# Three plain scatters and one accumulating scatter in each group of a message stream, on one NeuronCore

## What is computed

```python
h = jnp.maximum(_layernorm(x, axis=-1), 0.0)
x = x + _L0_gnn_ref(h, edge_index, W_l, W_r, b)          # mean over neighbours, two products, log-softmax
h = jnp.maximum(_layernorm(x, axis=-1), 0.0)
# second layer
weight = jnp.maximum(edge_rbf @ W1 + b1, 0.0) @ W2 + b2  # one row of 128 for each edge
hl = h @ Wl + bl
row, col = (edge_index[0], edge_index[1])                # row = src, col = dst
msg = hl[col] * weight
x = x + jax.ops.segment_sum(msg, row, num_segments=x.shape[0])
```

## Time and profile before

| | us |
|---|---|
| median of 3 runs | 3699.18 |
| the profiled execution's own time | 3703.27 |
| span of its trace (first to last instruction) | 3701.4 |
| first scatter starts | 1046.68 |
| last scatter starts | 3589.90 |
| POOL busy in the whole span | 2207.1 |

### The profile page before, as it was taken

One profiled execution on the slowest core, in us unless ns is written; L12 is line 12 of the kernel. 1 busy time (PEld: TensorE's weight loads), 2 busy tenths in 40 slices (PEclk: granted clock), 3 DMA queues, 4 the chain that ended last, 5 costly groups with the idle time before them and its releaser, 6 DMA issues.

```text
span 3701.4 us, 97235 instructions
## 1 busy us (share of the span) xinstructions
PE 3077.9 (83%) x26330; PEld 2498.3 (67%) x26331; DVE 2796.2 (76%) x7718; ACT 2089.7 (56%) x4907; POOL 2207.1 (60%) x1790
## 2 busy tenths in 40 slices
PE   1799999998677779888888888898888888888867
PEld 0699999997555557666666666666667766666656
DVE  8899999998855557886676766767677777877756
ACT  2699999994532235554454544554455545545546
POOL 4300101000357777777878787878878777878860
PEclk9999999998777779998998989999899999999989
DMA  3298998801034446766776666665677667767757
GB/s 110 70 337 315 319 319 316 316 7 36 12 70 88 88 104 162 175 157 145 151 154 152 135 145 145 154 154 132 144 166 173 161 147 172 172 141 165 174 118 207
DMA packets 576963, 592.90 MB, mean 160 GB/s; under 512 B 71050, under 2 KB 557954, under 8 KB 576689
## 3 DMA queue, kind: packets, MB, share of 16 engines
q1 hardware_dynamic: 449506, 470.49, 44.1%
q0 software_dynamic: 127184, 119.07, 18.2%
HBM read 293.94 MB, written 295.35 MB: 159 GB/s over the span
## 4 chain that ended last, share of the span: by engine, by line
PE 27%; DVE 26%; issue 18%; DMA 12%; POOL 11%; DVEq 5%; ACT 2%; SPq 0%; POOLq 0%; ACTq 0%
DMA messages<-big,idxr 11%; POOL messages L605 10%; PE PS L1120 10%; DVE X L1018 5%; PE PS L1111 5%; PE PS L1283 4%; DVE big L991 3%; DVE aux L769 3%; PE PS L1250 2%; DVE hpar L1007 2%; DVEq L1013 2%; DVE big L965 2%; DVE big L979 2%; PE PS L1262 2%; DVE big L968 1%
## 5 line engine op out<-in xcount | busy, mean ns | idle before, releaser
L605 POOL DMA_INDIRECT messages<-big,idxr x1664 | 2035.5, 1223 | 552.5 <-issue 462.4
L1283 PE MATMUL PS<-big,hpar 128*128 128x128 f32 x5120 | 677.5, 287 | 215.3 <-DVE hpar L1007 163.3
L1283 PEld LDWEIGHTS PS<-big,hpar 128*128 128x128 f32 x5120 | 623.8, 199 | 275.6 <-DVE hpar L1007 217.6
L1433 ACT ACTIVATE big<-PS,b1c 128x512 f32<-128x512 f32 x416 | 285.8, 687 | 788.5 <-PE PS L1239 788.5
L1018 DVE TENSOR_TENSOR X<-X,PS 128x128 f32 x1280 | 367.9, 287 | 315.3 <-issue 93.0
L1120 PE MATMUL PS<-h_parts,counts 128*128 128x258 f32 x3626 | 565.3, 296 | 0.0
L1360 ACT ACTIVATE counts<-PS 128x784 fp32r<-128x784 f32 x592 | 481.3, 825 | 94.3 <-PE PS L1111 85.2
L1250 PE MATMUL PS<-W2s,big 128*128 128x128 f32 x3328 | 524.3, 305 | 0.0
L1250 PEld LDWEIGHTS PS<-W2s,big 128*128 128x128 f32 x3328 | 439.5, 206 | 101.6 <-issue 101.6
L1444 ACT ACTIVATE big<-PS 128x512 f32<-128x512 f32 x416 | 247.5, 595 | 405.7 <-PE PS L1262 402.4
L1120 PEld LDWEIGHTS PS<-h_parts,counts 128*128 128x128 f32 x3626 | 469.6, 191 | 0.2 <-ACT counts L1360 0.2
(11 more groups left out here) (222 smaller groups left out, 3823.3 us busy)
## 6 DMA issues: line engine op xcount, KB each, us to landing
messages<-zeros SPq DMA_DIRECT2D x896, 193.5 KB
big<-messages SPq DMA_DIRECT2D x320, 516.0 KB
aux<-slot_rows SPq DMA_DIRECT2D x416, 128.0 KB
big<-in_edge_attr_dram SPq DMA_DIRECT2D x402, 128.0 KB
messages<-big,idxr POOLq DMA_INDIRECT x1664
X<-in_x_dram SPq DMA_DIRECT2D x12, 448.0 KB, 6.8
out_dram<-X SPq DMA_DIRECT2D x6, 448.0 KB
edge_places<-big SPq DMA_DIRECT2D x1, 2496.0 KB, 13.2
```

What stands on the lines that cost most here:

```text
L605: pool.indirect_dma_start(strm_d, bass.IndirectOffsetOnAxis(ap=idxr[:, n % U, j:j + 1], axis=0), outr[:, n % U, j, :], None, compute_op=AL ...
L1283: last = nc.tensor.matmul(to[:, r * C:(r + 1) * C], finhot[:, n % 2, r * 2 + q, :], fin[:, k, r, q * ROW:q * ROW + C], start=(q == 0), sto ...
```

## The change

The lists of accumulating slots change. In the first 400 groups, even groups keep one accumulating scatter (slot 1), and odd groups have one (slot 2) in place of two (slots 0 and 3). In the last 16 groups one (slot 1) in place of two (slots 1 and 3). The number of scatters, their sizes, their places, and every wait stay as they are. Accumulating scatters: before 6 in the first 4 groups, 594 in the loops and 32 in the last 16, together 632; after 416, one in each group. So 216 scatters become plain. The order of slots in two groups was plain, add, plain, plain, add, plain, plain, add; it becomes plain, add, plain, plain, plain, plain, add, plain.

```diff
-            def scatter(g, n, adding=(1, 3)):
+            def scatter(g, n, adding=(1,)):
...
                 for j in range(J):
                     pool.indirect_dma_start(strm_d, bass.IndirectOffsetOnAxis(ap=idxr[:, n % U, j:j + 1], axis=0),
                                             outr[:, n % U, j, :], None, compute_op=ALU.add if j in adding else ALU.bypass).then_inc(S_sc[n % U], 16)
 
-            fewer = ((1,), (0, 3))
+            fewer = ((1,), (2,))
             for g in range(U):
                 scatter(g, g, fewer[g % 2])
```

## The result

The changed kernel takes 3582.07 us (median of 4 runs, 3580.79 to 3582.44) against 3700.24 us for the kernel before in the same comparison: a ratio of 0.9678, 95% interval 0.9661 to 0.9695. That is 118 us less; 110 were forecast (3589 us, range 3568 to 3640). Two executions in a slower state are left out of every comparison: one of the six of experiment 10 (3892.75 us) and one of the kernel before beside it (5264.26 us).

The account below looks back on a forecast made before the run. POOL's issuing of scatters was taken as the bound; of 132 us saved there, stage terms 16, 22, 39, 8, 9, 1.5, 5 and 10 gave 110. From the profiled 3703.3 that is 3593, less 4.1 to the median: 3589 us, range 3568 to 3640.

Parts of the forecast that it names:

- What bounds: In the scatter stage of 2543 us POOL sets the pace, with 0.30 us between scatters; 2496 us are its own.
- The price of a conversion: On POOL, each accumulating scatter made plain saves 0.61 us (1.58 against 0.97); 216 of them save 132 us.
- No cost for longer runs of plain ones: In POOL's scatter stream, a third or fourth plain scatter in a row costs 0.97 us, like the second.
- Rival 3: POOL's scatters: a plain one after two plain ones backs up, at worst 130 us more, 3829 us; chance 0.08.
- rival 4: POOL's scatters: the 0.61 us is waiting for VectorE's port lock, so no change, 3699 us; no change in all 0.05.
- How much arrives: Over all stages of the scatter stream, 110 of POOL's 132 us reach the end, the rest limited by VectorE.
- Groups 64 to 103 and 328 to 367: Loops with an oct at each step: POOL catches up with VectorE, so 8 and 9 us come off, not 12.2 each.
- Groups 268 to 315: Loop with an oct at each step: POOL already waits 3.3 us for messages, so only 1.5 of 14.6 us comes off.
- well under 100 us: Sign of being right: VectorE's wait at L985, 203.2 us before, falls to well under 100 us.
- VectorE needs the same 6.1 us for a group as POOL: Where each step has an oct, VectorE's own time equals POOL's 6.1 us, leaving about 1 us of slack at L985.
- Rival 2: Scatter stream: TensorE and ScalarE become the wait, so only 65 us come off, 3634 us; chance 0.18 including cases towards the forecast.
- Rival 1: Scatter stream: VectorE speeds up with fewer DMA rows in the way, so all 132 us arrive, 3567 us; chance 0.07.

Follow-up runs that it names:

- experiment 10: The changed kernel run again, unchanged, for the spread of its runs: median 3584.26 us, ratio 0.9684 to the kernel before.
- experiment 5: Against the kernel before, the addition to X at L1018 cut to 8 of 128 columns (short sums): 3689.99 us, ratio 0.9972.
- experiment 3: Against the changed kernel, all scatters plain, no accumulating one left: 3463.72 us, ratio 0.9368 to the kernel before.
- experiment 7: Against the kernel before, two accumulating scatters (slots 1 and 3) in each of the 416 groups: 3811.30 us, ratio 1.0299.
- experiment 9: Against the changed kernel, all scatters plain and the addition to X at L1018 cut to 8 of 128 columns: 3373.43 us, ratio 0.9123 to the kernel before.
- experiment 4: Against the changed kernel, no accumulating scatter in odd groups, one still in even groups, last 16 groups unchanged: 3504.80 us, ratio 0.9476 to the kernel before.

## Why the prediction was right, point by point

**What bounds.** Right. "POOL sets the pace" rested on gaps of 0.30 us between scatters, and experiment 5 shows it: some 140 us less work for VectorE leave the stream where it was.

**The price of a conversion.** Right in kind, a tenth too high in the sum. 216 x 0.61 = 132 us was the term; POOL's busy time on L605 fell by 119.4 us, 0.55 us for each conversion (by 124.1 us in experiment 10, 0.57). By the mean of each kind, taken over all scatters of the timeline, plain ones stayed (0.990 us before and after), but the accumulating ones that are left rose from 1.605 to 1.635 us, 12 us for 416 of them (to 1.627 in experiment 10). Part of that is the median, 1.585 us before and 1.605 after (1.57 for one that stands behind a single plain one before, 1.60 now, and 1.60 behind four), part the share of long ones, which differs between profiles of the same kernel. The step that failed is small: I took the price of an accumulating scatter as a constant. Over all kernels here its median is 1.56 to 1.57 us where the last accumulating one stands next to it or one place away, and 1.59 to 1.62 us where two to seven plain ones lie between.

**No cost for longer runs of plain ones.** Right: 0.95 to 0.97 us as third and fourth in a row, and experiment 3 has a whole kernel of them. Rival 3 falls. So does rival 4 as the forecast put it, that the 0.61 us were waiting for VectorE: they follow the kind of scatter in every kernel here.

**How much arrives.** 110.4 us against a sum of 110. But this is two errors that nearly cancel, and so partly luck. POOL saves less than I counted, by 12 us (8 in experiment 10); and VectorE holds back less than I counted: some 10 us in place of 22. The stages in detail:

- *Groups 64 to 103 and 328 to 367.* The forecast had POOL catch up with VectorE, so that 8 and 9 us come off in place of 12.2 each. The measured 8.0 and 9.6 us fit for another reason. POOL never waits there in the changed kernel, not even at the end of a stage; all that it saves arrives, and it saves less than 12.2, since its scatters take 194.7 us in each of the two stages before, and 186.7 and 185.0 after. The distance between a message and its first scatter does shrink, from 10.2 us at group 64 to 3.7 at group 103, but it isn't used up. In these two stages the number was luck.
- *Groups 268 to 315.* I had 1.5 us, since POOL waited for messages there already, and they gave 6.1. POOL's scatters save 15.2 us, and its waits beyond the usual gap grow from 2.3 to 11.4. It is the only stage in which the changed kernel has such waits. Over half of them (5.5 and 0.9 us) stand at one turn of VectorE's loop, which the forecast had used for other loops alone:

```profile
2787.98 0.37 DVE L965 TENSOR_TENSOR big<-iotaB,blcol 128x200 bf16<-128x200 bf16 x1 [3.99 <-issue]
```

```profile
2792.33 0.96 POOL L605 DMA_INDIRECT messages<-big,idxr  x1 [5.76 <-DVE big L991]
...
2799.03 0.96 POOL L605 DMA_INDIRECT messages<-big,idxr  x1 [1.21 <-DVE big L991]
```

That it gave more than 1.5 us means that the producers got quicker, which the sum had left out. As an estimate, the stage's time and the fall of the distance in it (8.1 us before, 8.6 after) make 303.6 us for the producers before and 298.0 after. Two lines of VectorE account for most of it, 0.09 us a group for 48 groups; before, after:

```profile
L960 DVE TENSOR_SCALAR big<-aux,iotaP 128x512 bf16<-128x512 int16 x47 | 21.1, 449 | 0.0
...
L985 DVE CAST idxr<-big 128x4 int32<-128x4 f32 x47 | 10.6, 225 | 1.7 <-DMA messages<-big,idxr 1.5
```

```profile
L960 DVE TENSOR_SCALAR big<-aux,iotaP 128x512 bf16<-128x512 int16 x47 | 17.8, 378 | 0.0
...
L985 DVE CAST idxr<-big 128x4 int32<-128x4 f32 x46 | 9.4, 204 | 0.2
```

In groups 64 to 103 the two lines go from 470 and 305 ns to 402 and 277, and to 354 and 185 in experiment 3, while all other lines of VectorE stay within 0.03 us. That looks like a matter of how many scatters accumulate, but it isn't: with the lists of the kernel before and short sums (experiment 5) they take 387 and 225 ns, with four in eight accumulating (experiment 7) 439 and 269, and with none and short sums (experiment 9) again more:

```profile
L960 DVE TENSOR_SCALAR big<-aux,iotaP 128x512 bf16<-128x512 int16 x39 | 15.7, 403 | 0.0
...
L985 DVE CAST idxr<-big 128x4 int32<-128x4 f32 x38 | 10.8, 283 | 0.2
```

What the lengths follow is what POOL does when the instruction starts. In all twelve profiles an L960 that starts in a gap between two scatters takes 0.35 or 0.36 us in the mean and never over 0.43; one that starts while a scatter is issued takes 0.38 to 0.43 in the mean and up to 0.68 (0.55 where no scatter accumulates). For L985 it is 0.18 or 0.19 against 0.19 to 0.25 us in the mean. So the length hangs on where the beat of the two engines puts these instructions. The Trainium skill, "SBUF — State Buffer", section "Who interferes with whom", says that VectorE's casts and `tensor_scalar` can take a pair of ports that GpSimd needs too, that the one which comes second waits for the whole of the other, and that reductions don't contend. The trace agrees in which lines vary. It doesn't agree in the whole: the longest L960 is 0.34 us over the shortest, and no scatter is shorter than 0.95 us. In the prediction I had looked at that rule only from the side of POOL. That the ports are the cause is argued here and not shown.

**Where the size of the slack was misread.** VectorE's waits at L985 were expected "well under 100 us" after the change; they are 132.1. My own table has 58 us left in groups 0 to 51 alone (74.2 - 16), and the trace after has 58.6 there; the expectation contradicted the sum. And "VectorE needs the same 6.1 us for a group as POOL" in the stages with an oct at each step was too strong: experiment 3, where POOL waits for it, puts its own step at 5.8 to 5.9 us in groups 64 to 103 and 328 to 367 (234.7 / 40 and 232.0 / 40). That it walked in step with POOL for 40 groups was no proof that 6.1 us were its limit: the distance stays at 8.4 or 8.5 us from group 72 to 103, with 0.9 us of waits at L985 and L960 and L985 at their longest. What held it so exactly in step stays open. The forecast got by with it, since POOL stayed the bound there, at 5.8 to 5.9 us a group; for experiments 3 and 4 it made expectations some 50 and 35 us too timid. The reading "six to seven tenths" for the DMA engines holds, by and large, only from the first octs on; the row shows three and four tenths in the stage before them. Nothing in the sum rests on it.

**The other signs and rivals.** L605 has a mean of 1.152 us (1.14 forecast), the last scatter starts at 3470.2 and 3475.6 us in the two profiles (3480), and TensorE's granted clock is no lower (0.944 against 0.930). POOL begins to wait for L991 in one of the four loops with an oct at each step, where all four were forecast. Rival 2 (the producers' slack isn't real) falls: VectorE still waits 132.1 us at L985, and the loops with octs in three of four steps give 37.0 us, not 15. Rival 1 (all 132 us arrive) falls too, but part of its picture is true: the producers do get quicker in groups 268 to 315.

**The median.** Why the medians differ by 118 us where the stream gives 110 isn't settled. Part can be the start of the first scatter: the profiled run of the changed kernel began its stream early, that of the kernel before late, and of the others it isn't known. Part can be the stream itself, which differs by 4.4 us between two profiles of the changed kernel. The second series, with a profile that began late, gave 114 us. The forecast took the profiled execution's 4.1 us over the median off in full and didn't ask where they came from.

## What beats both

The kernel of experiment 3, with all scatters plain, takes 3463.72 us, a ratio of 0.9368 to the kernel before. Its bound where octs run is VectorE; groups 0 to 51 and the six written-out stretches still follow POOL at 5.1 to 5.2 us a group.

## What to carry to other kernels

When an engine's instructions follow each other with a constant small gap over a whole stage, it sets the pace even at a busy share of 60% on the page, and what an instruction gets cheaper by arrives until the next engine's own time is reached. That own time can't be read from an engine that runs beside the bound: VectorE took 6.1 us a group with next to no waits and could do 5.8. Its waits give a lower bound of the slack, and cutting the suspected work on one of the two engines tells which of them leads. A stall at the turn of a loop costs nothing while the buffer covers it, and has to be in the sum once it doesn't. Where a plain write leaves the same content as an accumulating one, take the plain one.

## What the runs showed of the hardware that I hadn't expected

- An indirect DMA that accumulates into DRAM costs POOL 1.56 to 1.62 us to issue in the median, a plain one of the same 128 rows of 516 bytes 0.96 to 0.99 us, and this difference hardly depends on what stands around it (kernels with 0 to 832 accumulating ones).
- The queue of these transfers has fewer packets with fewer accumulating ones, at the same bytes. Before and after:

```profile
q0 software_dynamic: 127184, 119.07, 18.2%
```

```profile
q0 software_dynamic: 102992, 119.07, 15.9%
```

216 conversions took away 24192 packets, 112 each. The sizes in the trace's packet records say why: an accumulating scatter sends each of its 128 rows by itself (80896 packets of 516 bytes before, 632 x 128), a plain one eight rows together (16512 of 4128 bytes, 1032 x 16). The forecast had no part of this. The last packet of a plain scatter ends 2.0 us after its issuing in the median, in both kernels, and that of an accumulating one 2.2 us before the change and 2.5 after; VectorE's waits shrank all the same.
- Two kinds of VectorE instruction (L960, L985) take up to twice and three times their shortest time (0.34 and 0.17 us) when they start while POOL issues an indirect DMA, and hardly more than it when they start between two.
